# Finding each node's last edge: from four passes over 2048 columns to one masked pass and a reduction

## What is computed

```python
edge_tgt = edge_index[1]                      # 16384 edges, each names one of 1024 nodes
eb = edge_attr @ We + be                      # (16384, 8)
col_bias = jnp.zeros((H, N), x.dtype).at[:, edge_tgt].set(eb.T)
scores = scores + col_bias[None, :, None, :]
```

## Time and profile before

| | before |
|---|---|
| median of three runs | 1240.35 us |
| profiled execution | 1236.63 us, its span 1234.4 us |
| TensorE busy | 1131.5 us (92%) |
| ScalarE busy | 1034.6 us (84%) |
| VectorE busy | 737.2 us (60%) |
| GpSimd busy | 117.8 us (10%) |

### The profile page before, as it was taken

How to read it: one execution, slowest core, us unless ns; L and a number is a source line. 1 busy time by engine, 2 the same in 40 slices (tenths; PEclk the granted TensorE clock), 3 DMA queues, 4 the chain that set the end, 5 groups by cost and what they waited for, 6 DMA issues and landing times. The chain is left out here.

```text
span 1234.4 us, 23587 instructions
## 1 busy us (share of the span) xinstructions
PE 1131.5 (92%) x8738; PEld 343.7 (28%) x8738; DVE 737.2 (60%) x1953; ACT 1034.6 (84%) x1124; POOL 117.8 (10%) x128
## 2 busy tenths in 40 slices
PE   2269999999999999999999999999999999899998
PEld 2022222222222222222222222222222222243332
DVE  8734365656565656565657575757565641567654
ACT  0059999999999999999999999999999999945553
POOL 4303010101010101000101000000000100000000
PEclk9999999999999999999999999999999999999999
DMA  1133131323131313131313132222222230022231
GB/s 39 53 79 82 37 84 45 81 49 81 49 80 50 80 50 80 49 80 50 80 51 79 50 77 53 68 55 77 59 66 57 58 85 4 14 64 69 65 85 48
DMA packets 61672, 75.96 MB, mean 62 GB/s; under 512 B 25988, under 2 KB 31108, under 8 KB 61532
## 3 DMA queue, kind: packets, MB, share of 16 engines
q1 hardware_dynamic: 59452, 73.78, 23.3%
q10 hardware_dynamic: 1600, 0.27, 0.1%
q0 software_dynamic: 480, 0.06, 0.1%
HBM read 37.47 MB, written 36.49 MB: 60 GB/s over the span
## 5 line engine op out<-in xcount | busy, mean ns | idle before, releaser
L1126 ACT ACTIVATE probs<-psum 128x1024 f32<-128x1024 f32 x1024 | 951.2, 1106 | 46.1 <-PE psum L1319 45.4
L1335 PE MATMUL psum<-probs,VA 128*32 128x512 f32 x4096 | 545.6, 605 | 8.2 <-DVE oT L1194 7.4
L1319 PE MATMUL psum<-QA,KA 54*128 54x512 bf16 x2048 | 349.4, 386 | 34.0 <-ACTq L1145 10.3
L1319 PEld LDWEIGHTS psum<-QA,KA 54*128 54x128 bf16 x2048 | 81.5, 93 | 535.7 <-ACT probs L1126 493.2
L1335 PEld LDWEIGHTS psum<-probs,VA 128*32 128x32 f32 x4096 | 82.6, 108 | 139.2 <-issue 105.1
L1194 DVE STREAM_TRANSPOSE oT<-psum 128x512 f32<-128x512 f32 x64 | 45.8, 715 | 122.9 <-PE psum L1335 122.2
L1161 ACT ACTIVATE probs<-psum,b 128x1024 f32<-128x1024 f32 x64 | 67.8, 1110 | 54.3 <-PE psum L1388 54.2
L1266 DVE TENSOR_TENSOR probs<-probs,psum 128x1024 f32<-128x1024 f32 x64 | 78.1, 1221 | 51.6 <-PE psum L1398 32.5
L1126 ACT ACT_TABLE_LOAD x1 | 1.3, 1283 | 72.4 <-issue 72.4
L1388 PE MATMUL psum<-m_x,w 64*128 64x512 f32 x256 | 60.5, 591 | 1.5 <-ACT probs L1161 1.5
L1412 PE MATMUL psum<-probs,w 128*64 128x512 f32 x256 | 60.9, 598 | 0.0
(11 more groups left out here) (182 smaller groups left out, 936.8 us busy)
## 6 DMA issues: line engine op xcount, KB each, us to landing
QA<-q_parts_d SPq DMA_DIRECT2D x64, 192.0 KB
KA<-k_parts_d SPq DMA_DIRECT2D x64, 192.0 KB
q_parts_d<-qk_parts SPq DMA_DIRECT2D x32, 192.0 KB, 2.5
k_parts_d<-qk_parts SPq DMA_DIRECT2D x32, 192.0 KB, 2.7
xT<-in_xT SPq DMA_DIRECT2D x16, 256.0 KB, 3.4
q_parts_d<-qk_parts SPq DMA_DIRECT2D x32, 128.0 KB, 2.7
k_parts_d<-qk_parts SPq DMA_DIRECT2D x32, 128.0 KB, 2.5
x_d<-x2T SPq DMA_DIRECT2D x16, 256.0 KB, 2.0
```

Of the source, the lines that this page charges most:

```text
L1126: nc.scalar.activation(probs[:, k % PROB_BUFS, :], score_buf(buf_of(k)), ACT.Exp).then_inc(exped, 1)
L1319: last = pe.matmul(score_buf(buf_of(k))[:, (g % 2) * BANK:(g % 2 + 1) * BANK], KA[rows_of(h, SCORE_ROWS), h // 2, jt * P:(jt + 1) * P], QA ...
L1335: last = pe.matmul(o_acc[32 * g:32 * g + 32, :], VA[:, jt, h, :], probs[:, k % PROB_BUFS, (g % 2) * BANK:(g % 2 + 1) * BANK], start=(jt == ...
```

## The change

Edge numbers are laid out the other way: an edge's number is now 128 x partition + column, so the partition, which the exponent tells, is the leading digit. The exponent field of the sums is kept in place as the high bits of a 32-bit word, and the column is written into its low bits. One pass does both (a bitwise and, then a bitwise or with `base`, which is now an integer array of column numbers that needs no constant added). The maximum of these words, read as floats, is the winner among the columns. What is left is arithmetic on 32 columns: the exponent and the column are taken apart, joined to an edge number, shifted by a constant, and set to zero where there is no edge. The one-hot inputs `node_af`, `node_bf` and `iota32` become bf16, for which a copy of `iota32` is added.

```diff
-        EDGE_CHAIN = 28
+        EDGE_CHAIN = 29
...
-            node_af = esb("node_af", [P, EC], F32)
-            node_bf = esb("node_bf", [P, EC], F32)
-            iota32 = esb("iota32", [P, 32], F32)
+            node_af = esb("node_af", [P, EC], BF16)
+            node_bf = esb("node_bf", [P, EC], BF16)
+            iota32f = esb("iota32f", [P, 32], F32)
+            iota32 = esb("iota32", [P, 32], BF16)
...
-            base = esb("base", [P, EC // 2 * 32], F32)
-            key = esb("key", [P, EC // 2 * 32], F32)
+            base = esb("base", [P, EC // 2 * 32], I32)
+            key = esb("key", [P, EC // 2 * 32], I32)
+            top4 = esb("top4", [P, 32], F32)
+            top_power = esb("top_power", [P, 32], I32)
+            top_column = esb("top_column", [P, 32], I32)
+            place = esb("place", [P, 32], F32)
...
-                    g.iota(base[:, :], pattern=[[2 * P, EC // 2], [0, 32]], base=0, channel_multiplier=0,
-                           allow_small_or_imprecise_dtypes=True).then_inc(base_ready, 1)
+                    g.iota(base[:, :], pattern=[[2, EC // 2], [0, 32]], base=0, channel_multiplier=0
+                           ).then_inc(base_ready, 1)
...
-                        v.memset(offset[32 * n:32 * n + 32, :], 64.0 * n - 62.5)
+                        v.memset(offset[32 * n:32 * n + 32, :], EC * (D * (n % 2) - 63.5) + n // 2 + 1.0)
...
+                    v.tensor_copy(iota32[:, :], iota32f[:, :])
                     v.tensor_copy(node_af[:, :], node_a[:, :])
                     v.tensor_copy(node_bf[:, :], node_b[:, :])
...
-                    v.wait_ge(base_ready, 1)
-                    link(v.tensor_scalar(base[:, :], base[:, :], offset[:, 0:1], None, ALU.add))
                     v.wait_ge(w_tok_loaded, 48)
...
                     v.wait_ge(edges_summed, 4)
-                    link(v.tensor_scalar(exps, sums.bitcast(I32), 23, None, ALU.logical_shift_right))
-                    link(v.scalar_tensor_tensor(key[:, :], exps, 0.5, base[:, :], ALU.mult, ALU.add))
-                    link(v.scalar_tensor_tensor(base[:, :], exps, 0.0, key[:, :], ALU.is_gt, ALU.mult))
-                    link(v.tensor_reduce(win4[:, :], base[:, :].rearrange("p (m b) -> p b m", b=32), AX.X, ALU.max))
+                    v.wait_ge(base_ready, 1)
+                    link(v.scalar_tensor_tensor(key[:, :], sums.bitcast(I32), POWER_BITS, base[:, :], ALU.bitwise_and,
+                                                ALU.bitwise_or))
+                    link(v.tensor_reduce(top4[:, :], key[:, :].bitcast(F32).rearrange("p (m b) -> p b m", b=32),
+                                         AX.X, ALU.max))
+                    v.tensor_scalar(top_power[:, :], top4[:, :].bitcast(I32), 23, None, ALU.logical_shift_right)
+                    link(v.tensor_scalar(top_column[:, :], top4[:, :].bitcast(I32), EC - 1, None, ALU.bitwise_and))
+                    link(v.scalar_tensor_tensor(place[:, :], top_power[:, :], EC / 2.0, top_column[:, :], ALU.mult, ALU.add))
+                    link(v.tensor_scalar(place[:, :], place[:, :], offset[:, 0:1], None, ALU.add))
+                    link(v.scalar_tensor_tensor(win4[:, :], top_power[:, :], 0.0, place[:, :], ALU.is_gt, ALU.mult))
                     link(v.transpose(win4T[:, :], win4[:, :]))
...
-        tgt=laid(np.asarray(L0_attn_edge_index)[1].reshape(EC, P).T), edge_attr=laid(L0_attn_edge_attr),
+        tgt=laid(np.asarray(L0_attn_edge_index)[1].reshape(P, EC)), edge_attr=laid(L0_attn_edge_attr),
```

More of the change, by code:

```diff
@@ L23 @@
 EPS = 1e-5
+POWER_BITS = 255 << 23
 BANK = 512
@@ L675, in attention @@
             weights_rest = esb("weights_rest", [P, W_COLS], F32)
-            exps = hot_a[:, :, :].rearrange("p m a -> p (m a)").bitcast(I32)
             sums = psum[:, 0:EC // 2 * 32]
@@ L763, in _ @@
                     prep_rstd, prep_rq, copy_v = pool_steps(g)
-                    g.iota(iota32[:, :], pattern=[[1, 32]], base=0, channel_multiplier=0,
+                    g.iota(iota32f[:, :], pattern=[[1, 32]], base=0, channel_multiplier=0,
                            allow_small_or_imprecise_dtypes=True).then_inc(iotas, 1)
```

## The result

| | before | after |
|---|---|---|
| median of ten runs | 1240.39 us | 1236.86 us |
| span of the profiled execution | 1234.4 us | 1234.4 us |
| VectorE busy | 737.2 us | 733.6 us |
| TensorE busy | 1131.5 us | 1131.4 us |

The ratio of the times is 0.9971, with a 95% interval of 0.9962 to 0.9981: faster by 3.5 us. The forecast was 1235.4 us, with a range from 1233.0 to 1238.0 us. The rival of the lost turn had 1237.2 us, and its mark is in the timeline. Yet the two profiled executions have the same span. Both facts need the trace.

A forecast was written before the change was run, and what follows sets the result against it. The prediction took one long VectorE chain in the prologue as the bound. Search -3.69, constant -1.32 and added copy +0.07 gave -4.94 us, so 1240.35 us became 1235.4 us, range 1233.0 to 1238.0 us.

The forecast's parts named there:

- the lost turn: Rival: in the prologue a cast loses its turn to GpSimd's memset of VA, losing 1.75 us; 1237.2 us, chance 0.18.
- the forecast's own range: Whole kernel: 1233.4 us, with a faster reduction and the runs' spread, to 1236.5 us, before widening for the lost turn.
- What bounds the kernel: Prologue: one long chain on VectorE from 2.6 us to 65.5 us, where the shift is handed to the queue.
- A microsecond for a microsecond: Each microsecond taken from VectorE before 65.5 us should move the first scores, and the end, by a microsecond.
- The passes: Search over 2048 columns: one elementwise pass of 2.29 us and a reduction of 3.57 us; whole search gains 3.69 us.
- the small steps: End of the search: five new operations on 128x32, 0.94 us in all, bounds 0.75 and 1.15 us.
- The constant: VectorE between hot_a and posb: the pass adding a constant to base goes whole, 1.32 us; TensorE's sums stay covered.
- The comparisons: One-hot comparisons in the prologue: bf16 inputs gain nothing, 4.42 us each; 2.30 us if at twice the rate.
- The added copy: Copy of iota32 ahead of two casts in the prologue: waits in GpSimd's shadow with them, costing 0.07 us.
- base as integers: GpSimd writes base as integers at the start: costed at nothing against 2.16 us, bounds 0.3 us either way.
- The sum: Whole change: -3.69 - 1.32 + 0.07 = -4.94 us, giving 1235.4 us from the median.
- The profile against the median: Profiled execution lies 3.7 us below the runs' median; the forecast was taken from the median, 1240.35 us.

The follow-up runs named there:

- again: The changed kernel run and profiled once more, unchanged, on the faster chip: 1233.55 us, ratio 0.9974.
- copy_first: The changed kernel with the copy of iota32 moved ahead of the wait for the targets: 1232.49 us, ratio 0.9960.
- step_one: copy_first with both comparisons reading 32 neighbouring elements again and again, in place of one element 32 times: 1228.20 us, ratio 0.9929.
- bf16_alone: The kernel before with only node_af, node_bf and iota32 in bf16 and the added copy; old search: 1238.60 us, ratio 1.0013.
- room: copy_first with GpSimd's base and memsets held back until the casts are done, and scaling after both comparisons: 1233.35 us, ratio 0.9946.
- search_only: The changed kernel with node_af, node_bf and iota32 in f32 again and no copy of iota32: 1235.60 us, ratio 0.9963.

## Why the prediction was right, and where it was not

The measured 1236.86 us lies outside the forecast's own range, 1233.4 to 1236.5 us. It lies inside the stated range because that had been widened to take in the lost turn, which is what happened. So the rival's mechanism, and not the forecast's, gave the time.

*What bounds the kernel.* Right. The full part is as long as before, TensorE busy 1131.4 and 1131.5 us, and what VectorE wins before the shift arrives at the first scores: 3.33 us by `again`. "A microsecond for a microsecond" at the end is right to within the clock: `again` lost 0.2 us, `copy_first` 1.1 us of 5.26 us. The prediction allowed for nothing after the first scores.

*The passes.* The masked pass took 2.28 us (2.29 forecast), the reduction 3.57 us (3.57), the small steps 1.03 us from 33.25 us to the transpose (0.94). The one that adds `offset` took 0.24 us and not 0.18 us. A gain of 3.62 us in place of 3.69 us.

*The constant.* Gone, 1.32 us. The sums of TensorE stayed hidden: the last group of them started at 21.99 us and took 0.57 us, and the search started at 27.34 us, so 4.8 us of cover were left where 5.2 us had been worked out.

*The comparisons.* 4.42 us, as taken, and `step_one` shows that the reason given was the right one: 2.29 us once the input is read in order, at the price of 2.30 us that had been worked out.

*The added copy.* This step failed. It was costed at 0.07 us, since "a third one beside them waits in the same shadow". It cost a turn of the next memset: `hot_b` came 1.65 us late (5.97 to 7.62 us). The rival had 1.75 us for it and 0.18 of the chance; `copy_first` and `bf16_alone` show it from both sides. The argument for the forecast, that the second of two operations had gone through in both places of the trace, said nothing of a third. The gap of 0.06 us between GpSimd's instructions should have weighed more.

*base as integers.* 2.05 us and not 2.16 us, a gain of 0.09 us at `hot_b` in `copy_first`, inside the bounds of 0.3 us.

*The sum.* -3.62 - 1.32 + 1.65 = -3.29 us. `v_new` moved by 3.29 us on the faster chip (48.96 to 45.67 us) and by 3.35 us on the slower ones. The timed runs say 3.1 and 3.5 us. The measured 1236.86 us lies closer to the lost turn's 1237.2 us than to the forecast's 1235.4 us.

*The profile against the median.* The 3.7 us between them were taken as an offset that the change leaves alone. That was right, but the reason was not known: 3.5 us of wait behind the gathers, which the slower chips have and the faster one has not.

## What to carry to other kernels

A short operation added to a queue is not free because its neighbours are waiting anyway: where VectorE and GpSimd take turns, look at which instruction of the other engine comes next, and how long it is. Better still, order the long memsets of GpSimd behind the short casts of VectorE, beside work that doesn't mind them; that was worth 2.5 us here (`v_new` at 44.93 us in `room`, 47.42 us in `search_only`; 2.25 us by the medians), half of what the new search and the dropped pass save. And the narrower type for the two inputs of an operation paid here only where each input was read element after element.

## What was not expected of the hardware

On two of three chips the eight gathers delay the start of `v_new` by 3.5 us (5.06 against 1.56 us) in each of the kernels profiled there with eight gathers, and with one gather it is 1.55 us. `v_new` follows the end of the last gather's issue there, by 1.3 to 1.5 us. How the one holds the other isn't shown.

Beside TensorE's reads in steps of 128 bf16 elements, VectorE and GpSimd were slower on other tiles of SBUF by a factor of 2.6 to 4.9 (2.85 against 1.11 us, 3.40 against 0.69 us), both at once. The cause is inferred from the overlap.

A scattered write cost VectorE what a scattered read did: 3.60 us for 2048 elements, against 2.28 us, as the reduction took 3.57 against 2.29 us.

The granted clock of the profile read 1.00 while groups of 8 matmuls took 1.93 us and later 1.07 us.
